# Broadcasts moved to the head of each slot, norm rows joined, and transpositions in 64-row halves, in a software-pipelined MetaFormer block

## The chip, the cores and the metric

The kernel runs on one core of one Trainium2 chip. The metric is device time in microseconds (us) of one execution; a change of less than about 0.2% can't be told from none here. The median of the kernel before is 706.19 us.

## The reference, cut to what matters

The input `x` is 4 images of 64 channels and 128 x 128 tokens. All arithmetic is in float32.

```python
def ln_c(v):                                   # over the channels
    return (v - v.mean(1)) / sqrt(v.var(1) + 1e-6)
xn = ln_c(x)
k, q = relu(Wk @ xn + bk), relu(Wq @ xn + bq)  # 8 heads of 8 channels
v = Wv @ xn + bv
context = einsum('bhkn,bhvn->bhkv', k, v)      # summed over a whole image
x1 = x + Wr @ einsum('bhkv,bhkn->bhvn', context, q) + br
t = tokens(x1)                                 # 64 channels each
n = (t - mean(t)) / sqrt(var(t) + 1e-5)
top_p, top_i = top_k(softmax(n @ router_w + router_b), 2)    # 8 experts
out = t + sum over 2 of top_p / sum(top_p) * (n @ expert_w[top_i] + expert_b[top_i])
```

## The kernel before, in words

**Tiles.** 128 partitions hold 64 channels of two stretches of an image (`s` = 0, 1). A group is 1024 tokens of each, as two units `u` of 512; there are 32 groups, 8 for each image. Of the eight PSUM banks six (`misc`) rotate: `bank_uses()` lists every use of a bank in TensorE's order, use number i has bank i mod 6, and TensorE waits (`when_free`) until the use six places back was read (`taken`).

**Steps and slots.** A loop over steps `n` runs every stage of the work on another group: the stage that lags by L steps works on group `n - L`. Each step has four slots `k`, and each engine has its own list of what it issues in a slot, in order; an engine never goes past an instruction that waits.

- Slot 3, lag 0: `measure_x` makes the rows of means and squares of x (L986), ScalarE copies them to `stat_rows` (L497). Step after, slot 0: `to_columns` turns them back (2 transpositions, L1006), ScalarE copies to `xs` (L504), and VectorE's seven small `x_deviations` (L654 to L657, `newton` at L642 to L644) give 1/deviation.
- Lag 2: slot 0 `turn_x`, 8 transpositions of 128 x 128, four for each unit (L911); VectorE `normalise`s each unit (L676) into `xnT`; slot 1 `turn_back` transposes 8 times again (L921) and ScalarE copies to `xn` (L492).
- Lag 3: slot 0 `make_keys` (L936, L943), slot 1 `sum_up` of keys against `xnT` (L974) and `add_sums` on VectorE (L688), slot 2 `make_queries` (L960). At the end of an image four `fold` steps build the attention matrix (L1030 to L1036).
- Lag 11: slot 2 `attend` (L1020) and `residual` on VectorE (L720), slot 3 `square_x1` on ScalarE. Lag 12: `route` makes the rows of the second norm and the router (L986), lag 13 their columns.
- From lag 14: 27 small VectorE steps (`gates`) choose two experts for two groups at once; `quad_in` and `gates_by_phase` lay them on eight slots, `gate_steps` lays ScalarE's square root, exponential and casts. Lag 16, slot 3: `turn_gates` (L1045), ScalarE copies to `grows` (L565).
- Lag 17, two iterations `i` in each slot (8 for a group): `broadcast(i)` spreads gate rows over 64 partitions each, two banks (L1059); for s = 0 VectorE multiplies with `x1d` out of PSUM (L816, `product`), for s = 1 ScalarE copies the bank to `gbs` (L571) and GpSimd multiplies (L431); `experts(i)` adds both products with the expert weights into `out_bank` (L1073, L1076). At the end of a unit VectorE's `result` (L826) adds x1, and SP stores. The first matmul of the next unit (L1070) waits for that.

**Order within a slot, before.** TensorE: the stages' own work, then `broadcast` for the next slot's iterations, then `experts` of this slot's. VectorE: fold, result, sums, `x_deviations`, residual, gates, `normalise`, and the slot's two products last. ScalarE: keys, columns, back, rows, then `copy_gates`, then the rest. GpSimd: the two products, and in slot 1 the squares of the next x.

Of the kernel before, what the change touches and what calls it, by code (L numbers as in the profile page):

```python
# [31 lines left out]
NLG = SE + 2 * S  # L32

# [7 lines left out]
L_COLS, L_TURN, L_KEYS, L_AGAIN, L_ATTEND, L_ROUTE, L_GATES, L_TURN_GATES, L_EXPERTS = 1, 2, 3, 9, 11, 12, 14, 16, 17  # L41
# [3 lines left out]
R_X, R_Q, R_X1, R_Z = 3, 8, 7, 4  # L45
# [17 lines left out]

def bank_uses():

    for n in range(STEPS):
        for k in range(SLOTS):
            if folding(n, k):
                yield "fold", *folding(n, k)
            if k == 0:  # L70
                if real(n - L_KEYS):
                    yield from (("keys", n - L_KEYS, s) for s in range(S))
                if real(n - L_COLS):
                    yield "stat_cols", n - L_COLS, 0
                if real(n - L_ROUTE - L_COLS):
                    yield "route_cols", n - L_ROUTE - L_COLS, 0
                if real(n - L_TURN):
                    yield from (("turned", n - L_TURN, u) for u in range(U))
            if k == 1:
                if real(n - L_KEYS):  # L80
                    yield "sums", n - L_KEYS, 0
                if real(n - L_TURN):
                    yield from (("back", n - L_TURN, u) for u in range(U))
# [5 lines left out]
            if k == 3:  # L89
                if real(n - L_TURN_GATES):  # L90
                    yield "gate_rows", n - L_TURN_GATES, 0
                if real(n):
                    yield "stat_rows", n, 0
                if real(n - L_ROUTE):
                    yield "route_rows", n - L_ROUTE, 0
            for i in iterations(n, k + 1):
                yield from (("spread", i, s) for s in range(S))
# [6 lines left out]
def constants():  # L104
# [15 lines left out]
    for s in range(S):  # L120
        for k, col in enumerate((0, S, SE, SE + S)):
            means[half == s, k, col + s] = 1.0 / C
# [14 lines left out]
def metaformer_block(nc, x, Wk, bk, Wq, bq, Wv, bv, Wr, br, router_w, router_b, expert_w, expert_b,  # L137
# [4 lines left out]
    with ExitStack() as ctx:  # L142
# [44 lines left out]
        stat_rows = sb("stat_rows", [P, U, P])  # L187
# [17 lines left out]
        route_rows = sb("route_rows", [P, U, P])  # L205
# [182 lines left out]
        def quad_in(n, k, phase):  # L388

            p, late = divmod(SLOTS * (n - L_GATES) + k - 1 - phase, 2 * SLOTS)  # L390
# [3 lines left out]
        def _(pool):  # L394
# [20 lines left out]
            def square_x(g, u):  # L415

                if u == 0:
                    pool.wait_ge(x_in[g % R_X], 32 * (g // R_X + 1))
                    if g:
                        when_filled(pool, ("stat_rows", g - 1, 0))  # L420
# [46 lines left out]
        def _(act):  # L467
# [17 lines left out]
            def take_back(g, u):  # L485

                bank = when_filled(act, ("back", g, u))
# [4 lines left out]
                nc.scalar.copy(xn[:, g % 2, u * NT:(u + 1) * NT], bank[:, :]).then_inc(taken_of(("back", g, u)), 1)  # L492

            def take_stat_rows(g):

                bank = when_filled(act, ("stat_rows", g, 0))
                nc.scalar.copy(stat_rows[:, :, :].rearrange("p u n -> p (u n)"), bank[:, 0:U * P]  # L497
                               ).then_inc(taken_of(("stat_rows", g, 0)), 1)

            def take_stat_cols(g):  # L500

                bank = when_filled(act, ("stat_cols", g, 0))
                upto(act, xstat_dve, g * N_XSTAT)
                nc.scalar.copy(xs[:, :, :], bank[:, 0:U * P].rearrange("p (a r) -> p a r", r=W)[:, :, 0:2 * S]  # L504
                               ).then_inc(taken_of(("stat_cols", g, 0)), 1)
# [6 lines left out]
            def take_route_rows(g):  # L512

                bank = when_filled(act, ("route_rows", g, 0))
                nc.scalar.copy(route_rows[:, :, :].rearrange("p u n -> p (u n)"), bank[:, 0:U * P]
                               ).then_inc(taken_of(("route_rows", g, 0)), 1)

            def take_route_cols(g):

                bank = when_filled(act, ("route_cols", g, 0))  # L520
                upto(act, gate_dve, (g // 2 - 2) * N_GATE + 8)
                half = g % 2 * U * NJ
                nc.scalar.copy(lg[:, g // 2 % 2, half:half + U * NJ, :],
                               bank[:, 0:U * P].rearrange("p (a r) -> p a r", r=W)[:, :, 0:NLG]
                               ).then_inc(taken_of(("route_cols", g, 0)), 1)

            def square_x1(g, u):

                when_taken(act, ("attended", g, u))
                if g:  # L530
                    when_filled(act, ("route_rows", g - 1, 0))
# [41 lines left out]
            gate_steps = {0: root_dev, 5: exponent, 7: high, 8: low}  # L573
# [16 lines left out]
            for n in range(STEPS):  # L590
                if n == L_TURN:
                    spread_key_bias()
                for k in range(SLOTS):
                    if k == 0:
# [3 lines left out]
                        if real(n - L_COLS):  # L598
                            take_stat_cols(n - L_COLS)
                        if real(n - L_ROUTE - L_COLS):  # L600
                            take_route_cols(n - L_ROUTE - L_COLS)
                    if k == 1 and real(n - L_TURN):
                        for u in range(U):
                            take_back(n - L_TURN, u)
                    if k == 3:
                        if real(n - L_TURN_GATES):
                            take_gate_rows(n - L_TURN_GATES)
                        if real(n):
                            take_stat_rows(n)

                    for i in iterations(n, k + 1):
                        copy_gates(i)

                    if k == 1 and real(n - L_COLS):
                        root_x(n - L_COLS)
                    if k == 2 and real(n - L_KEYS):
                        for s in range(S):
                            take_queries(n - L_KEYS, s)
                    if k == 3:
                        if real(n - L_ROUTE):  # L620
                            take_route_rows(n - L_ROUTE)
                        if real(n - L_ATTEND):
                            for u in range(U):
                                square_x1(n - L_ATTEND, u)
                    for phase, step in gate_steps.items():
# [4 lines left out]
        def _(dve):  # L630
# [18 lines left out]
            def x_deviations(g, k0, k1):  # L649
# [11 lines left out]
                for k in range(k0, k1):  # L661
                    if k == 0:
                        when_taken(dve, ("stat_cols", g, 0))
# [6 lines left out]
            def normalise(g, u):  # L670

                bank = when_filled(dve, ("turned", g, u))
# [3 lines left out]
                dve.tensor_tensor(xnT[:, g % 2, u, :, 1:P + 1].rearrange("p j (s c) -> p j s c", s=S),  # L676
                                  bank[:, :].rearrange("p (j s c) -> p j s c", j=NJ, s=S),
                                  halves(rstd[:, g % 2, u, :]).unsqueeze(3).to_broadcast([P, NJ, S, C]), ALU.mult
                                  ).then_inc(taken_of(("turned", g, u)), 1)
# [43 lines left out]
            def gates(p, k0, k1):  # L723
# [7 lines left out]
                def start():  # L731
                    for i in range(2):
                        when_taken(dve, ("route_cols", 2 * p + i, 0))
# [73 lines left out]
            gates_by_phase = {8: (26, 27), 0: (0, 4), 2: (4, 9), 3: (9, 12), 4: (12, 16), 6: (16, 20), 7: (20, 26)}  # L807
# [63 lines left out]
            for n in range(STEPS):  # L871
                if n == L_TURN:
                    set_weights()
                for k in range(SLOTS):
# [4 lines left out]
                    if k == 1:  # L879
                        if real(n - L_KEYS):  # L880
                            add_sums(n - L_KEYS)
                        if real(n - L_COLS):
                            x_deviations(n - L_COLS, 0, 4)
                    if k == 2:
                        if real(n - L_EXPERTS):
                            result(n - L_EXPERTS, 0)
                        if real(n - L_ATTEND):
                            for u in range(U):
                                residual(n - L_ATTEND, u)
                    if k == 3 and real(n - L_COLS):  # L890
                        x_deviations(n - L_COLS, 4, N_XSTAT)
                    for phase, (k0, k1) in gates_by_phase.items():
                        if quad_in(n, k, phase) is not None:
                            gates(quad_in(n, k, phase), k0, k1)
                    if k == 0 and real(n - L_TURN):
                        for u in range(U):
                            normalise(n - L_TURN, u)

                    for i in iterations(n, k + 1):
                        product(i)  # L900
# [3 lines left out]
        def _(pe):  # L904

            def turn_x(g, u):

                use = ("turned", g, u)
                bank = when_free(pe, use)
# [3 lines left out]
                ins.then_inc(filled_of(use), 1)  # L913

            def turn_back(g, u):

                use = ("back", g, u)
                bank = when_free(pe, use)
                when_taken(pe, ("turned", g, u))
# [249 lines left out]
```

## Time and profile before

| | |
|---|---|
| three runs | 705.63 to 706.54 us, median 706.19 |
| the profiled execution | 708.03 us, of which the span from the first to the last instruction is 706.2 |
| mean granted TensorE clock | 0.990 |
| busy: TensorE, VectorE, ScalarE, GpSimd | 647.4, 532.2, 428.5, 396.5 us |

Busy time of TensorE is the union of its matmuls; pipelined matmuls overlap at their ends, so starts, not durations, give the pace. "PEld" is the load of the stationary operand.

### The profile page before, as it was taken

The numbers are of one execution on the slowest core, as the hardware profiler recorded it, in microseconds if no ns is written. First come the engines' busy times: TensorE is split into PE (matmuls) and PEld (weight loads), VectorE is DVE, ScalarE is ACT, GpSimd is POOL, SyncE is SP. The second block draws the span as 40 slices with busy tenths as digits, with TensorE's granted clock in tenths as the row PEclk, the third lists the DMA queues.
The fourth block names the chain that finished last, engine by engine and source line by source line (L and its number), as shares of the span: only waits on it lengthen the run. The fifth ranks groups of instructions, "written<-read, shape, count | busy, mean of one in ns | idle before, by whom it ended". The sixth has DMA issues, their size and how long they took to land.

```text
span 706.2 us, 20616 instructions
## 1 busy us (share of the span) xinstructions
PE 647.4 (92%) x7846; PEld 302.0 (43%) x7846; DVE 532.2 (75%) x1176; ACT 428.5 (61%) x852; POOL 396.5 (56%) x350
## 2 busy tenths in 40 slices
PE   3898999799999999999999999999989889896786
PEld 1676766444544444444544444444322223231221
DVE  3443456878788988888788988867889998978853
ACT  2354556857566676657576776756656666564542
POOL 7132342165456566565456566555657667575785
PEclk9999999999999999999999999999999999999999
DMA  6232544655565555555566564444656555454442
GB/s 141 61 75 71 130 122 122 169 145 123 136 151 135 136 140 125 127 136 123 133 150 148 123 148 99 98 111 107 149 130 152 120 120 135 102 131 97 107 104 46
DMA packets 32660, 86.16 MB, mean 122 GB/s; under 512 B 7650, under 2 KB 7826, under 8 KB 32562
## 3 DMA queue, kind: packets, MB, share of 16 engines
q1 hardware_dynamic: 32082, 84.64, 50.7%
q8 instruction: 63, 1.03, 0.7%
q0 software_dynamic: 288, 0.19, 0.1%
q14 instruction: 35, 0.29, 0.1%
q10 hardware_dynamic: 192, 0.01, 0.0%
HBM read 34.47 MB, written 16.78 MB: 73 GB/s over the span
## 4 chain that ended last, share of the span: by engine, by line
PE 68%; DVE 13%; ACT 10%; issue 7%; DMA 1%; POOL 1%; DVEq 0%; SPq 0%; ACTq 0%; POOLq 0%
PE bank L1073 25%; PE bank L1059 8%; PE bank L986 5%; PE bank L921 5%; PE bank L974 5%; PE bank L943 4%; PE bank L911 4%; ACT grows L565 3%; DVE z L816 3%; PE bank L1020 3%; PE bank L1006 2%; ACT L543 2%; DVE osb L826 2%; PE bank L1070 2%; DVE x L720 2%
## 5 line engine op out<-in xcount | busy, mean ns | idle before, releaser
L431 POOL TENSOR_TENSOR z<-gbs,x1d 128x512 f32<-128x512 f32 x256 | 320.6, 1275 | 220.7 <-ACT gbs L571 164.8
L1076 PE MATMUL bank<-z,ew 128*64 128x512 f32 x512 | 248.0, 607 | 0.0
L1073 PE MATMUL bank<-z,ew 128*64 128x512 f32 x512 | 247.9, 607 | 0.0
L571 ACT COPY gbs<-bank 128x512 f32<-128x512 f32 x256 | 140.0, 593 | 95.3 <-PE bank L1059 94.4
L816 DVE TENSOR_TENSOR z<-bank,x1d 128x512 f32<-128x512 f32 x256 | 162.9, 677 | 20.4 <-PE bank L1059 20.1
L1059 PE MATMUL bank<-grows,sel 64*64 64x512 f16 x1024 | 89.3, 388 | 28.2 <-DVE z L816 17.0
L422 POOL TENSOR_TENSOR xsq<-xin 128x512 f32<-128x512 f32 x64 | 65.6, 1046 | 81.8 <-DMA xin<-in_x_dram 78.2
L1073 PEld LDWEIGHTS bank<-z,ew 128*64 128x64 f32 x512 | 65.7, 138 | 105.6 <-issue 95.8
L492 ACT COPY xn<-bank 128x512 f32<-128x512 f32 x64 | 34.6, 588 | 68.2 <-PE bank L921 68.2
L676 DVE TENSOR_TENSOR xnT<-bank,rstd 128x512 f32<-128x512 f32 x64 | 41.3, 684 | 39.2 <-PE bank L911 37.0
L1059 PEld LDWEIGHTS bank<-grows,sel 64*64 64x64 f16 x1024 | 24.1, 104 | 97.2 <-issue 34.4
L1076 PEld LDWEIGHTS bank<-z,ew 128*64 128x64 f32 x512 | 65.6, 138 | 0.0
L826 DVE TENSOR_TENSOR osb<-bank,x 128x512 f32<-128x512 f32 x64 | 43.8, 685 | 23.1 <-PE bank L1076 23.1
L565 ACT COPY grows<-bank 128x1024 f16<-128x1024 f16 x32 | 32.3, 1010 | 30.3 <-PE bank L1045 30.3
L474 ACT ACTIVATE keys<-bank 128x512 f32<-128x512 f32 x64 | 34.8, 595 | 25.4 <-PE bank L943 25.4
L720 DVE SCALAR_TENSOR_TENSOR x<-bank,br_col,x_again 128x512 f32<-128x512 f32 x64 | 44.9, 743 | 5.2 <-PE bank L1020 4.8
L482 ACT ACTIVATE q<-bank,bq_col 128x512 f32<-128x512 f32 x64 | 40.6, 689 | 7.2 <-PE bank L960 7.2
L974 PEld LDWEIGHTS bank<-xnT,keys 128*64 128x64 f32 x1024 | 34.7, 139 | 13.3 <-issue 12.2
L974 PE MATMUL bank<-xnT,keys 128*64 128x66 f32 x1024 | 36.7, 225 | 1.2 <-ACT keys L474 1.0
L921 PE MATMUL bank<-k,xnT 128*128 128x128 f32 x256 | 35.9, 284 | 1.7 <-DVE xnT L676 1.2
L532 ACT ACTIVATE x1sq<-x 128x512 f32<-128x512 f32 x64 | 37.4, 645 | 0.0
L943 PEld LDWEIGHTS bank<-wk_bd,xn 64*64 64x64 f32 x2048 | 35.5, 135 | 4.2 <-issue 1.9
(138 smaller groups left out, 885.0 us busy)
## 6 DMA issues: line engine op xcount, KB each, us to landing
x1d<-x SPq DMA_DIRECT2D x128, 256.0 KB, 4.5
xin<-in_x_dram SPq DMA_DIRECT2D x64, 256.0 KB, 4.1
x_again<-in_x_dram SPq DMA_DIRECT2D x64, 256.0 KB, 4.1
out_dram<-osb SPq DMA_DIRECT2D x128, 128.0 KB, 2.4
k<-in_const_dram SPq DMA_DIRECT2D x1, 453.5 KB, 3.7
ew_nat<-in_L_ffn_expert_w_dram POOLq DMA_DIRECT2D x2, 64.0 KB, 6.5
sel<-in_const_sel_dram SPq DMA_DIRECT2D x1, 128.0 KB, 3.5
bk_rows<-bk_wide ACTq DMA_DIRECT2D x6, 1.0 KB, 1.7
```

The source lines that it names most:

```text
L422: pool.tensor_tensor(xsq[:, u * NT:(u + 1) * NT], half, half, ALU.mult).then_inc(x_squared, 1)
L431: pool.tensor_tensor(z[:, 1, i % R_Z, :], gbs[:, i % R_Z, :], x1d[:, g % 2, 1, u * NT:(u + 1) * NT], ALU.mult).then_inc(z_pool, 1)
L571: nc.scalar.copy(gbs[:, i % R_Z, :], bank[:, :]).then_inc(taken_of(("spread", i, 1)), 1)
L720: dve.scalar_tensor_tensor(x1[:, g % R_X1, half], bank[:, :], br_col[:, 0:1], x_again[:, g % 2, half], ALU.add, ALU.add).then_inc(taken_of ...
L816: dve.tensor_tensor(z[:, 0, i % R_Z, :], bank[:, :], x1d[:, g % 2, 0, u * NT:(u + 1) * NT], ALU.mult).then_inc(taken_of(("spread", i, 0)), 1)
L826: dve.tensor_tensor(osb[:, g % 2, half], out_bank[:, :], x1[:, g % R_X1, half], ALU.add).then_inc(out_done, 1)
L921: ins = pe.transpose(bank[:, j * P:(j + 1) * P], xnT[:, g % 2, u, j, 1:P + 1], eye)
L943: ins = pe.matmul(banks[s][C * a:C * a + C, j * C:(j + 1) * C], xn[rows, g % 2, j * P + C * a:j * P + C * a + C], wk_bd[rows, rows], start ...
L974: ins = pe.matmul(bank[C * s:C * s + C, 0:C + 2], keys[:, s, at:at + C], xnT[:, g % 2, u, j, C * s:C * s + C + 2], start=(u == 0 and j == ...
L1059: ins = pe.matmul(bank[cols, :], sel[rows, j, cols], grows[rows, g % 2, u * NT:(u + 1) * NT], start=True, stop=True)
L1073: pe.matmul(out_bank[0:C, :], ew[:, j, :], z[:, 0, i % R_Z, :], start=False, stop=(j == PAIRS - 1), skip_group_check=True).then_inc(prod_d ...
L1076: pe.matmul(out_bank[C:P, :], ew[:, j, :], z[:, 1, i % R_Z, :], start=False, stop=(j == PAIRS - 1), skip_group_check=True).then_inc(prod_d ...
```

## The change

1. **Order in a slot.** TensorE issues `broadcast` first, before folds and stages. ScalarE's `copy_gates` comes first too. VectorE: fold, result, `x_deviations` and the gate steps 26, 0 to 3 and 4 to 6 (`gates_first`, these from SBUF but for 26) before the products; `normalise`, `add_sums`, `residual` and the other gate steps behind them. In slot 1 `turn_back` now comes before `sum_up`.
2. **Gates two slots later**, `turn_gates` at lag 17, slot 1, and the experts at lag 18: 50 steps where there were 49, with eight buffers of `x1` for seven.
3. **Joined rows.** Rows of x and of x1 go to one bank, one `rows_sb` and one pair of transpositions: where both exist one ScalarE copy and two transpositions less per step.
4. **Halves.** `turn_x` and `turn_back` transpose 64 rows at a time, 16 transpositions of 64 rows by 128 columns of which the two row halves alternate and write two banks. Both banks are full only at the end, and `normalise` and `take_back` work on a row half in place of a unit.

```diff
@@ bank_uses, and the same order in the TensorE loop @@
+            for i in iterations(n, k + 1):
+                yield from (("spread", i, s) for s in range(S))
             if folding(n, k):
...
-            for i in iterations(n, k + 1):
-                yield from (("spread", i, s) for s in range(S))
@@ VectorE loop @@
+                    for phase, (k0, k1) in gates_first.items():
+                        if quad_in(n, k, phase) is not None:
+                            gates(quad_in(n, k, phase), k0, k1)
+                    for i in iterations(n, k + 1):
+                        product(i)
+                    if k == 0 and real(n - L_TURN):
+                        for s in range(S):
+                            normalise(n - L_TURN, s)
+                    if k == 1 and real(n - L_KEYS):
+                        add_sums(n - L_KEYS)
+                    if k == 2 and real(n - L_ATTEND):
...
-            gates_by_phase = {8: (26, 27), 0: (0, 4), 2: (4, 9), 3: (9, 12), 4: (12, 16), 6: (16, 20), 7: (20, 26)}
+            gates_first = {8: (26, 27), 0: (0, 4), 2: (4, 7)}
+            gates_by_phase = {2: (7, 10), 3: (10, 11), 4: (11, 16), 5: (16, 18), 6: (18, 24), 7: (24, 26)}
-            gate_steps = {0: root_dev, 5: exponent, 7: high, 8: low}
+            gate_steps = {0: root_dev, 4: exponent, 7: high, 8: low}
@@ TensorE @@
-            def turn_x(g, u):
...
-                for j in range(NJ):
-                    ins = pe.transpose(bank[:, j * P:(j + 1) * P],
-                                       xin[:, g % R_X, u * NT + j * P:u * NT + (j + 1) * P], eye)
+            def turn_x(g):
+                uses = [("turned", g, s) for s in range(S)]
+                banks = [when_free(pe, use) for use in uses]
+                for a in range(U * NJ):
+                    for s in range(S):
+                        rows = slice(C * s, C * s + C)
+                        ins = pe.transpose(banks[s][:, a * C:(a + 1) * C], xin[rows, g % R_X, a * P:(a + 1) * P],
+                                           eye[rows, rows])
+                        if a == U * NJ - 1:
+                            ins.then_inc(filled_of(uses[s]), 1)
...
+            def to_columns(n):
...
+                when_taken(pe, ("rows", n, 0))
                 for u in range(U):
-                    ins = pe.transpose(bank[:, u * P:(u + 1) * P], rows[:, u, :], eye)
+                    ins = pe.transpose(bank[:, u * P:(u + 1) * P], rows_sb[:, u, :], eye)
...
                     if k == 1:
+                        if real(n - L_TURN_GATES):
+                            turn_gates(n - L_TURN_GATES)
+                        if real(n - L_TURN):
+                            turn_back(n - L_TURN)
                         if real(n - L_KEYS):
                             sum_up(n - L_KEYS)
```

## Rows read from the trace of the kernel before

**Rows 1.** The page: busy time, and the chain that ended last.

```profile
PE 647.4 (92%) x7846; PEld 302.0 (43%) x7846; DVE 532.2 (75%) x1176; ACT 428.5 (61%) x852; POOL 396.5 (56%) x350
...
PE 68%; DVE 13%; ACT 10%; issue 7%; DMA 1%; POOL 1%; DVEq 0%; SPq 0%; ACTq 0%; POOLq 0%
```

**Rows 2.** Three stretches: window, length, busy us of each engine, clock, DMA, GB/s.

```profile
0.00:142.40 142.40, 122.66 (x2225) 82.45 (x2225) 71.31 (x230) 75.54 (x170) 46.61 (x64) 0.99 0.47 113
142.40:439.40 297.00, 291.92 (x3670) 140.07 (x3672) 247.97 (x541) 197.99 (x398) 180.12 (x151) 1.00 0.56 133
439.40:706.20 266.80, 232.77 (x1953) 79.48 (x1949) 212.91 (x408) 154.98 (x286) 169.77 (x136) 0.98 0.49 115
```

**Rows 3.** TensorE's timeline in a full step: start, us, engine, line, shapes, count.

```profile
301.91 1.10 PE L943 MATMUL bank<-wk_bd,xn 64*64 64x64 f32 x64
...
303.22 0.38 PE L1006 MATMUL bank<-k,route_rows 128*128 128x128 f32 x2
303.43 1.04 PE L911 MATMUL bank<-k,xin 128*128 128x128 f32 x8
304.40 0.63 PE L1059 MATMUL bank<-grows,sel 64*64 64x512 f16 x8
...
313.16 0.60 PE L1059 MATMUL bank<-grows,sel 64*64 64x512 f16 x6
...
314.31 0.41 PE L1070 MATMUL bank<-grows,eb_rows 128*64 128x512 f16 x2
...
318.24 0.61 PE L986 MATMUL bank<-x1sq,k 128*32 128x256 f32 x8
318.95 0.63 PE L1059 MATMUL bank<-grows,sel 64*64 64x512 f16 x8
319.50 0.64 PE L1073 MATMUL bank<-z,ew 128*64 128x512 f32 x1
```

**Rows 4.** Timeline of an early step, TensorE and VectorE.

```profile
62.28 1.09 PE L960 MATMUL bank<-xn,wq 64*64 64x512 f32 x8
...
65.84 1.04 PE L911 MATMUL bank<-k,xin 128*128 128x128 f32 x8
66.48 1.29 DVE L676 TENSOR_TENSOR xnT<-bank,rstd 128x512 f32<-128x512 f32 x2 [2.72 <-PE bank L911]
68.00 1.09 PE L921 MATMUL bank<-k,xnT 128*128 128x128 f32 x8
69.02 1.09 PE L960 MATMUL bank<-xn,wq 64*64 64x512 f32 x8
```

**Rows 5.** ScalarE's timeline: gate rows in slot 3 of steps 39, 40 and 41.

```profile
569.09 1.01 ACT L565 COPY grows<-bank 128x1024 f16<-128x1024 f16 x1
586.06 1.01 ACT L565 COPY grows<-bank 128x1024 f16<-128x1024 f16 x1 [2.24 <-PE bank L1045]
599.11 1.01 ACT L565 COPY grows<-bank 128x1024 f16<-128x1024 f16 x1
```

**Rows 6.** Timeline of step 40, TensorE and VectorE.

```profile
579.76 1.19 DVE L777 TENSOR_TENSOR bstat<-bstat,lg 128x32 f32<-128x32 f32 x1
...
582.16 0.41 PE L1059 MATMUL bank<-grows,sel 64*64 64x512 f16 x4 [1.49 <-DVE z L816]
```

**Rows 7.** Line L777: durations in ns, min/median/max.

```profile
L777 DVE TENSOR_TENSOR bstat<-bstat,lg x16: 191/192/1195, 116.0 to 641.4; 128x32 f32<-128x32 f32 x16
```

**Rows 8.** Columns as in rows 2, three microseconds of step 42.

```profile
614.00:617.00 3.00, 3.00 (x9) 0.49 (x5) 2.86 (x8) 0.00 (x0) 1.86 (x2) 0.50 0.39 87
```

**Rows 9.** Two pairs of weight loads, from the timeline of PEld.

```profile
178.04 0.29 PEld L1032 LDWEIGHTS bank<-wvT,sT_sb 64*128 64x128 f32 x2 [0.81 <-ACT q L482]
...
302.94 0.20 PEld L1006 LDWEIGHTS bank<-k,stat_rows 128*128 128x128 f32 x2
```

**Rows 10.** ScalarE's timeline: rows of x in slot 3 of steps 14 and 16.

```profile
118.94 0.37 ACT L497 COPY stat_rows<-bank 128x256 f32<-128x256 f32 x1
...
140.85 0.41 ACT L497 COPY stat_rows<-bank 128x256 f32<-128x256 f32 x1
```

More of the change, by code:

```diff
@@ L32 @@
 NLG = SE + 2 * S
+NROW = NLG + 2 * S
 PPB = HW // (S * NP)
@@ L88, in bank_uses @@
                     yield from (("queries", n - L_KEYS, s) for s in range(S))
[L89 to L95, printed above, removed]
-            for i in iterations(n, k + 1):
-                yield from (("spread", i, s) for s in range(S))
+            if k == 3 and has_rows(n):
+                yield "rows", n, 0
 ROUND = 6
@@ L593, in _ @@
                 for k in range(SLOTS):
+                    for i in iterations(n, k + 1):
+                        copy_gates(i)
                     if k == 0:
@@ L878, in _ @@
                         result(n - L_EXPERTS - 1, 1)
[L879 to L889, printed above, removed]
+                    if k == 1 and real(n - L_COLS):
+                        x_deviations(n - L_COLS, 0, 4)
+                    if k == 2 and real(n - L_EXPERTS):
+                        result(n - L_EXPERTS, 0)
                     if k == 3 and real(n - L_COLS):
                         x_deviations(n - L_COLS, 4, N_XSTAT)
+                    for phase, (k0, k1) in gates_first.items():
+                        if quad_in(n, k, phase) is not None:
+                            gates(quad_in(n, k, phase), k0, k1)
+                    for i in iterations(n, k + 1):
+                        product(i)
[5 more added lines that the diff above has]
+                    if k == 2 and real(n - L_ATTEND):
+                        for u in range(U):
+                            residual(n - L_ATTEND, u)
                     for phase, (k0, k1) in gates_by_phase.items():
@@ L894, in _ @@
                             gates(quad_in(n, k, phase), k0, k1)
[L895 to L900, printed above, removed]
             result(GROUPS - 1, 1)
@@ L977, in sum_up, with make_rows @@
                 ins.then_inc(filled_of(use), 1)
-            def rows_of(use, tile, squares, w, w_square):
+            def make_rows(n):
+                use = ("rows", n, 0)
                 bank = when_free(pe, use)
-                outs = [bank[W * j:W * (j + 1), 0:U * P].rearrange("p (u n) -> p u n", u=U) for j in range(NJ)]
-                for moving, weights, start in ((tile, w, True), (squares, w_square, False)):
-                    chunks = moving.rearrange("p (u j n) -> p u j n", u=U, j=NJ)
+                parts = []
+                if real(n):
+                    pe.wait_ge(x_in[n % R_X], 32 * (n // R_X + 1))
+                    pe.wait_ge(x_squared, (n + 1) * U)
+                    parts += [(xin[:, n % R_X, :], mean_w), (xsq[:, :], square_w)]
+                g = n - L_ROUTE
+                if real(g):
+                    pe.wait_ge(x1_squared, (g + 1) * U)
+                    parts += [(x1[:, g % R_X1, :], route_w[:, :]), (x1sq[:, :], route_square_w)]
+                for part, (tile, weights) in enumerate(parts):
+                    chunks = tile.rearrange("p (u j n) -> p u j n", u=U, j=NJ)
@@ L985, in rows_of @@
                     for j in range(NJ):
-                        ins = pe.matmul(outs[j], weights, chunks[:, :, j, :], start=start, stop=not start,
-                                        skip_group_check=True)
+                        out_rows = bank[W * j:W * (j + 1), 0:U * P].rearrange("p (u n) -> p u n", u=U)
+                        ins = pe.matmul(out_rows, weights, chunks[:, :, j, :], start=(part == 0),
+                                        stop=(part == len(parts) - 1), skip_group_check=True)
@@ L1103, in _ @@
                 for k in range(SLOTS):
+                    for i in iterations(n, k + 1):
+                        broadcast(i)
                     if folding(n, k):
```

179 lines of the change are left out of this document (76 added, 103 removed).

## The prediction

> **What bounds the kernel now.** I read the page first: TensorE is busy 92% of the span and makes 68% of the chain that ended last, but a fifth of that chain is VectorE and ScalarE [rows 1]. A share like that hides stages, so I cut the span into three by the experts' start and the last group's entry [rows 2]. Steps 0 to 16 (up to 142.4) have no experts: TensorE is busy 123 of 142 us, most of the rest at the start. Steps 17 to 31 are full: 297 us for 15 steps, 19.8 each, TensorE busy 98%, VectorE 16.5 us a step. From 439.4 the x stages drain and 17 steps take 266.8 us, TensorE 87% and VectorE 80% busy.
>
> Then the timelines. In a full step TensorE is never idle for long, but two places are slack although they look busy, because the ends of pipelined matmuls cover them. The two broadcasts of a slot take 0.55 us (318.95 to the experts at 319.50), in slot 2 they take 1.15 (313.16 to 314.31): 0.60 lost, for the banks which `residual` frees. And the last rows matmul, 0.43 long by its neighbours' spacing, starts at 318.24, the broadcast only at 318.95: 0.28 lost, for `grows` [rows 3]. An early step, 6.74 us (62.28 to 69.02), has no gap: VectorE starts on the first unit at 66.48 while TensorE still transposes the second, is done at 67.77, and `sum_up` fills the time until `turn_back` at 68.00 [rows 4]. A late step takes 17.0 or 13.0 us by turns (569.09, 586.06, 599.11), 30.0 a pair [rows 5]. The long ones are even: there VectorE has most gate steps ahead of its products, and TensorE waits 1.49 us for a product's bank [rows 6]. Some of these small SBUF steps last 1.19 us where their median is 0.19 [rows 7]; in the timeline the long ones lie beside a GpSimd product. In step 42, after the same two waits, TensorE's granted clock is at the lower level, 1.2 GHz, for at least 3 us [rows 8].
>
> **Halved transpositions.** 8 transpositions of 128 moving columns take 0.97 us from start to next start (303.43 to 304.40), 0.107 each and some 0.1 for the change of shape [rows 3]. With 64 moving columns and the row halves side by side a pair should take 0.055: that matmuls of 64 columns in four quarters of the array keep such a pace is seen at L943, 64 of them in 1.03 us (301.91 to 302.94), 0.064 for four [rows 3]. The question is the weight load, which keeps 128 columns. The load pair of L1006, transpositions, lasts 0.20 with 0.14 for one, so it starts 0.06 apart; that of L1032, ordinary float32 weights of 64 rows by 128 columns, 0.29 with 0.18 for one, starts 0.11 apart [rows 9]. The nearest row is the transposition's: I take 0.055 a pair, 8 x (0.107 - 0.055) = 0.42 us less for each of `turn_x` and `turn_back`, 0.84 a step. Bounds: nothing, if loads of a pair follow one another or take 0.11; and +0.85 each (16 x 0.11 = 1.76) if the halves neither load nor multiply side by side and each load takes 0.11.
>
> The Trainium skill ("TensorE: Matmul & The Clock Gate", LDWEIGHTS) has the load's time go by its columns alone, 128 / 1.2 = 107 ns, however few the rows. By it a pair takes 0.107 and the turns save nothing. The trace agrees for L1032 and not for L1006 [rows 9].
>
> **Joined rows.** The rows' matmuls stay. The second pair of transpositions, 0.21 us (303.22 to 303.43) [rows 3], goes in steps where both exist, 13 to 31. The ScalarE copy that goes is hidden anyway.
>
> **Broadcasts first, gates later.** In a full step the 0.60 and the 0.28 go: the broadcasts' banks were read a slot earlier, and `grows` is copied two slots ahead. So TensorE alone would need 19.70 - 0.88 - 0.21 - 0.84 = 17.8. But VectorE has 16.5 a step [rows 2], with its order against it. In slot 0 both halves of `normalise` (1.29) start only after all of `turn_x`; `x_deviations` follow, then slot 1's products, and `turn_back` needs the bank of the first: I draw 0.3 us of waiting in odd steps, 0.7 in even ones. `add_sums` now stands behind `turn_back` and `sum_up` and blocks VectorE for about 1.2 us; in even steps six gate steps (2.5 us) queue behind it, then `result` and slot 2's products, and `make_queries` waits about 0.8 to 1.6 for their bank. Odd steps 18.1, even 19.7; 19.0 with what long SBUF steps add. 14 full steps (one fewer) make 266 where 15 made 297: **-31**.
>
> **Early steps.** Here the move of `turn_back` costs. Only `to_columns` (about 0.25) lies between it and `turn_x`. VectorE starts when all 16 are done, works 1.29, and `turn_back` starts some 1.2 us late, with nothing of TensorE's to cover it. Net +1.2 - 0.84 = +0.36, in steps 2 to 14: +4.7, less 0.4 for the join. Steps 15 and 16 took 21.9 us with gates in them [rows 10]; now 15, 16 and 17 have them, VectorE-bound at about 10.6 each, 32: +10. Together **+14.3**: full steps start near 156.7.
>
> **Late steps, 32 to 49.** TensorE needs 12.7 (the 13.0 of an odd step less its waits), VectorE was busy 212.9 / 17 = 12.5 a step over all late steps [rows 2], the last of which lack gates and `residual`; where it has them I take 13.4, an estimate. But its gate steps now lie behind the products and more evenly over slots (at most 2.5 us in one). I draw one chain left: even slot 1's gates, `result` in slot 2, the first matmul of the next unit; about 2.3 us a pair. 13.9 a step for 35 to 42, so 27.8 a pair where it was 30.0 [rows 5]. Steps 32 to 34: 18.2, 17.6, 16.3. Step 43: 12.6; 44 to 46: 12.5 each, VectorE's gates; 47 to 49: 10.8 each, near what GpSimd's 8 products need (169.8 / 17 = 10.0 [rows 2]), and 2 for the end. Sum 52.1 + 111.2 + 12.6 + 37.5 + 34.4 = 247.8, against 266.8: **-19**.
>
> Sum: 14.3 - 31 - 19 = -35.7. The profiled execution took 708.0 and would take 672.3; it is 1.8 over the median, so 670.5 for the median, say **670**.
>
> **Hidden at nothing.** The stores, loads and x1d copies move in SP's queue with their conditions, each a step ahead of its reader; DMA is about half busy in all three stretches [rows 2]. Moving `copy_gates` first on ScalarE costs nothing while ScalarE has a third of its time free; `exponent`, one slot earlier, waits for the last gate step of its own slot and holds the next slot's copies about 0.7 us, covered by the slot between a product and its experts. If that cover is gone TensorE waits the 0.7 once in 2 steps: 11 us in all.
>
> **Rivals.**
> - *Turns save nothing* (loads 0.11 a pair or one after another). For: L1032's load; by the Trainium skill's rule on load columns (TensorE page, LDWEIGHTS) this is what happens. Against: L1006's. Early steps +0.84 x 15 = 12.6; full steps 19.5, as VectorE's chain hides part, +7: **690**. Chance 0.2.
> - *VectorE stays the bound.* Its chains cost in every step what they cost in even ones: full steps 19.6 (+8), late pairs 30.0 (+9): **687**. For: 16.5 us busy in a full step, and the blocked `add_sums`. Against: most gate steps now leave the way of the products. Chance 0.13.
> - *Slower: the halves serialise.* A turn of 1.76 us instead of 0.5, 64 turns, +1.25 each, 80 us less what full and late steps hide: **about 730**. It decides from 1.05 us a turn on, against 0.97 before: (706 - 670) / 64 = 0.56 over my 0.5. For: no row shows transpositions of 64 rows. Against: L943's four quarters. Chance 0.05.
> - *Better than drawn.* The waits of slots 1 and 2 do not come, full steps 18: **655**. Chance 0.1.
>
> The forecast has 0.52. Its own range is 661 to 680. Within 0.2%, which is what a measurement here can tell, lies almost none: 0.02; slower 0.06 (the third rival and an unseen wait), faster 0.92. Leaving out the last rival's lower half and the slower one, the range is 654 to 693.
>
> **What would show it.** After: 16 transpositions in about 0.5 us, loads in pairs; an early step near 7.1 us with TensorE waiting about 1.2 for `normalise`; full steps near 19.0 with waits at `turn_back` and `make_queries` in even ones, none at broadcasts; late pairs near 28; fewer falls of the clock. Wrong it would be by the turn's length first, worth 6.4 us for each 0.1, then by the early wait, 1.2 x 15 = 18 us.

## The result and the profile after

The changed kernel takes 749.92 us (746.78 to 751.62, 4 runs), the kernel before 706.37 us (705.63 to 708.09, 4 runs): ratio 1.0604, 95% interval 1.057 to 1.0637. It is 43.5 us slower where 36 us less was forecast. In order: the page of the profiled execution (span 747.2 us), then its three stages, cut at the same work as in [rows 2] (the rows' copies of steps 17 and 31, before of 16 and 31).

```profile
PE 642.1 (86%) x8318; PEld 283.8 (38%) x8318; DVE 534.8 (72%) x1176; ACT 421.5 (56%) x832; POOL 398.4 (53%) x350
...
PE 56%; DVE 26%; issue 10%; ACT 4%; DVEq 0%; ACTq 0%
```

```profile
0.00:156.60 156.60, 122.36 (x2647) 78.36 (x2647) 77.82 (x249) 80.95 (x181) 50.57 (x68) 0.98 0.44 109
156.60:464.20 307.60, 273.47 (x3616) 123.01 (x3618) 233.13 (x508) 181.18 (x359) 169.57 (x141) 0.95 0.50 120
464.20:747.20 283.00, 246.27 (x2057) 82.45 (x2053) 223.90 (x421) 159.40 (x296) 178.26 (x143) 0.95 0.48 114
```

No engine has much more work; TensorE is idle for 105 us where it was for 59, and VectorE's share of the chain doubled [rows 1]. The mean clock fell from 0.990 to 0.958: (1 - 0.958) x 2 x 747.2 = 63 us at the 1.2 GHz level, 14 before. The forecast had 156.7, 266 and 247.8 for the stages: the first is right to 0.1 us, the second 41.6 too short, the third 35.2.

An ordinary full step, TensorE's timeline, as in [rows 3]:

```profile
271.09 0.40 PE L1059 MATMUL bank<-grows,sel 64*64 64x512 f16 x2
271.90 0.41 PE L1059 MATMUL bank<-grows,sel 64*64 64x512 f16 x4 [0.40 <-DVE z L806]
272.49 0.40 PE L1059 MATMUL bank<-grows,sel 64*64 64x512 f16 x2 [0.18 <-DVE z L806]
272.71 0.41 PE L936 MATMUL bank<-bk_rows,ones 64*64 64x512 bf16 x4
...
273.98 0.71 PE L905 MATMUL bank<-k,xin 64*128 64x64 f32 x16
274.62 0.44 PE L1006 MATMUL bank<-k,rows_sb 128*128 128x128 f32 x2
274.99 0.41 PE L1070 MATMUL bank<-grows,eb_rows 128*64 128x512 f16 x2
...
290.56 0.63 PE L1059 MATMUL bank<-grows,sel 64*64 64x512 f16 x8
```

A turn takes 0.64 us start to start (273.98 to 274.62). From L936 to the next step's broadcasts TensorE has no wait: 17.85 us, and with these broadcasts (290.56 to the next L936 at 291.02) 18.3. But the broadcasts at the head of this step, an odd one (23), take 1.6 (271.09 to 272.71), for banks that products hold. The even step behind it waits 0.40 us before `turn_x` and 1.12 before `make_queries`, and not before `turn_back`. Ordinary pairs of full steps took 39.4, forecast 37.8 to 38.0, before 39.3.

The worst place is a step that folds. Step 27, TensorE and VectorE in order of time, and below it TensorE's clock (0.57) from 356 to 364:

```profile
354.46 0.41 PE L1059 MATMUL bank<-grows,sel 64*64 64x512 f16 x4 [1.49 <-DVE z L806]
...
357.45 0.64 PE L936 MATMUL bank<-bk_rows,ones 64*64 64x512 bf16 x4 [1.62 <-issue]
...
364.29 0.63 PE L1059 MATMUL bank<-grows,sel 64*64 64x512 f16 x8
...
364.84 0.43 PE L1036 MATMUL bank<-wrT,ctxT_sb 64*128 64x64 f32 x2
...
365.31 0.29 DVE L696 COPY att<-bank 128x128 f32<-128x128 f32 x1 [3.14 <-PE bank L1036]
365.44 2.48 POOL L430 TENSOR_TENSOR z<-gbs,x1d 128x512 f32<-128x512 f32 x2 [7.29 <-ACT gbs L563]
365.52 1.21 DVE L642 SCALAR_TENSOR_TENSOR xstat<-xs 128x16 f32<-128x16 f32 x1
...
366.76 1.19 DVE L643 TENSOR_TENSOR xstat<-xstat,xs 128x16 f32<-128x16 f32 x1
...
370.33 1.28 DVE L806 TENSOR_TENSOR z<-bank,x1d 128x512 f32<-128x512 f32 x2
...
371.07 1.12 PE L919 MATMUL bank<-k,xnT 64*128 64x64 f32 x16 [5.25 <-DVE z L806]
```

```profile
356.00:364.00 8.00, 6.55 (x96) 4.10 (x96) 3.23 (x6) 1.60 (x5) 2.15 (x2) 0.57 0.20 43
```

VectorE is in its list at the fold's last step (L696), whose TensorE half now stands behind the broadcasts. It waits 3.14 us, then `x_deviations` come out while GpSimd multiplies (1.21 and 1.19 us for steps that take 0.17 otherwise), and only then the product, at 370.33, whose bank `turn_back` needs: TensorE idles 5.25 us. The pair of steps 18 and 19 took 54.7 us, 26 and 27 took 56.1, where other full pairs take 39.4: 32 us. Before, a pair with folds cost 1.3 more than another. Steps 34 and 35 hold folds too.

A late even step, the end of slot 2 and slot 3 of step 40:

```profile
614.93 0.63 PE L1059 MATMUL bank<-grows,sel 64*64 64x512 f16 x8
...
615.71 0.43 DVE L788 TENSOR_TENSOR bank<-bank,bstat 128x256 f32<-128x256 f32 x1
...
616.18 1.07 ACT L544 CAST gT<-bank 128x256 f16<-128x256 f32 x2 [3.56 <-DVE bank L788]
...
617.14 1.09 ACT L563 COPY gbs<-bank 128x512 f32<-128x512 f32 x2
617.35 0.70 DVE L738 TENSOR_TENSOR bank<-bank,gT 128x512 f32<-128x512 f32 x1 [1.21 <-ACT gT L544]
...
617.96 1.23 DVE L723 SCALAR_TENSOR_TENSOR bstat<-lg 128x32 f32<-128x32 f32 x1
...
620.93 1.22 DVE L806 TENSOR_TENSOR z<-bank,x1d 128x512 f32<-128x512 f32 x2
...
621.61 0.41 PE L1059 MATMUL bank<-grows,sel 64*64 64x512 f16 x4 [2.85 <-DVE z L806]
```

ScalarE's cast (`high`) stands at the end of slot 2 and waits for gate steps 24 and 25 of that same slot, which now stand behind its products. So it waits 3.56 us, holds slot 3's copy of the gates (its broadcasts stand ready from about 615.5, the copy starts at 617.14), and VectorE waits for it in turn at step 26, ahead of slot 3's products; then steps 0 to 3 lie beside GpSimd's product. TensorE waits 2.85. From step 36 on late pairs took 31.3 to 32.7, forecast 27.8, before 30.0 [rows 5] and, from step 40 on, 31.7.

### The profile page after: what moved, and what is told of

Read it like the earlier page. It is cut to its first block, busy times and chain, and to the rows that moved or that the text cites. A ratio compares the mean times of both kernels' runs of the same rounds, so it can differ in the third digit from the quotient of the medians.

```text
span 747.2 us, 21530 instructions
## 1 busy us (share of the span) xinstructions
PE 642.1 (86%) x8318; PEld 283.8 (38%) x8318; DVE 534.8 (72%) x1176; ACT 421.5 (56%) x832; POOL 398.4 (53%) x350
## 4 chain that ended last, share of the span: by engine, by line
PE 56%; DVE 26%; issue 10%; ACT 4%; DVEq 0%; ACTq 0%
PE bank L1073 18%; PE bank L1059 6%; DVE z L806 6%; PE bank L974 5%; PE bank L996 5%; PE bank L960 3%; PE bank L919 3%; PE bank L943 3%; PE bank L1070 3%; PE bank L905 3%; PE bank L1020 3%; DVE x L709 2%; DVE bstat L766 2%; DVE bstat L723 2%; DVE osb L816 2%
## 5 line engine op out<-in xcount | busy, mean ns | idle before, releaser
L1076 PE MATMUL bank<-z,ew 128*64 128x512 f32 x512 | 252.8, 618 | 0.0
L1073 PE MATMUL bank<-z,ew 128*64 128x512 f32 x512 | 252.7, 618 | 0.0
L563 ACT COPY gbs<-bank 128x512 f32<-128x512 f32 x256 | 138.4, 591 | 151.1 <-PE bank L1059 150.9
L1073 PEld LDWEIGHTS bank<-z,ew 128*64 128x64 f32 x512 | 67.6, 142 | 99.6 <-issue 81.7
L664 DVE TENSOR_TENSOR xnT<-bank,rstd 128x512 f32<-128x512 f32 x64 | 41.2, 685 | 55.0 <-PE bank L905 53.7
L1059 PEld LDWEIGHTS bank<-grows,sel 64*64 64x64 f16 x1024 | 21.1, 105 | 139.2 <-issue 100.5
L1076 PEld LDWEIGHTS bank<-z,ew 128*64 128x64 f32 x512 | 67.6, 142 | 0.0
L919 PE MATMUL bank<-k,xnT 64*128 64x64 f32 x512 | 24.5, 238 | 27.8 <-DVE xnT L664 14.8
L960 PE MATMUL bank<-xn,wq 64*64 64x512 f32 x256 | 35.3, 621 | 6.3 <-DVE z L806 6.3
L1020 PE MATMUL bank<-q,att 64*64 64x512 f32 x256 | 35.3, 627 | 5.6 <-issue 5.6
L943 PEld LDWEIGHTS bank<-wk_bd,xn 64*64 64x64 f32 x2048 | 38.7, 145 | 3.3 <-issue 0.5
L974 PE MATMUL bank<-xnT,keys 128*64 128x66 f32 x1024 | 39.5, 234 | 0.0
```

The costliest lines, as they stand in the source:

```text
L563: nc.scalar.copy(gbs[:, i % R_Z, :], bank[:, :]).then_inc(taken_of(("spread", i, 1)), 1)
L943: ins = pe.matmul(banks[s][C * a:C * a + C, j * C:(j + 1) * C], xn[rows, g % 2, j * P + C * a:j * P + C * a + C], wk_bd[rows, rows], start ...
L960: ins = pe.matmul(banks[s][cols, :], wq_4[rows, cols], xn[rows, g % 2, u * NT:(u + 1) * NT], start=True, stop=True)
L974: ins = pe.matmul(bank[C * s:C * s + C, 0:C + 2], keys[:, s, at:at + C], xnT[:, g % 2, u, j, C * s:C * s + C + 2], start=(u == 0 and j == ...
L1059: ins = pe.matmul(bank[cols, :], sel[rows, j, cols], grows[rows, g % 2, u * NT:(u + 1) * NT], start=True, stop=True)
L1073: pe.matmul(out_bank[0:C, :], ew[:, j, :], z[:, 0, i % R_Z, :], start=False, stop=(j == PAIRS - 1), skip_group_check=True).then_inc(prod_d ...
```

## The experiments

The result and its trace left three theories of the 80 us between forecast and result: the gate steps set ahead of the products (A), `turn_back` ahead of `sum_up` (B), the broadcasts ahead of the folds (C). Each experiment has its ratio to the kernel before as timed beside it (median 706.14 us for e1 to e4, 705.06 for e5 to e8, 705.35 for e9 to e12).

**e1: all gate steps behind the products.**

```diff
-            gates_first = {8: (26, 27), 0: (0, 4), 2: (4, 7)}
-            gates_by_phase = {2: (7, 10), ...
+            gates_by_phase = {8: (26, 27), 0: (0, 4), 2: (4, 10), ...
```

> The changed kernel with gate steps 26, 0 to 3 and 4 to 6 behind the slot's products, as all others (x_deviations stay ahead). Theory A (these steps, with the wait for ScalarE's casts in step 26 and the SBUF steps that meet GpSimd's products, hold the products of every second step's slot 3, so that TensorE waits 2 to 3 us for banks and its clock falls): waits of L1059 for L806's product fall from 24 us to under 8, time at the low clock from some 63 us to under 25, time 715 to 725. Theory B (turn_back ahead of sum_up is what costs, early and in fold steps): 745 to 750, early step still 7.2 us. Theory C (fold behind the broadcasts): 740 to 750, steps 18, 19, 26 and 27 still 27 us each.

760.14 us (755.65 to 762.06), ratio 1.0784 (1.0743 to 1.0826): slower by 10. Theory A falls: ahead of the products is the better place for them. The size is not of the place alone, for step 26, which ScalarE's `low` waits for, moved too; e11 below moves the others without it.

**e2: `sum_up` ahead of `turn_back` again**, in TensorE's loop and the banks' order.

```diff
+                        if real(n - L_KEYS):
+                            sum_up(n - L_KEYS)
                         if real(n - L_TURN):
                             turn_back(n - L_TURN)
-                        if real(n - L_KEYS):
-                            sum_up(n - L_KEYS)
```

> The changed kernel with sum_up ahead of turn_back again, in TensorE's order and in the order of banks. Theory B: the early step goes from 7.2 to about 6.3 us (15 of them, 13 us), the 5 us waits of turn_back in fold steps shrink, 720 or less. Theory A: only the early steps gain, 733 to 738, late steps unchanged at about 31.5 a pair.

730.66 us (727.13 to 731.24), ratio 1.0375 (1.035 to 1.04): 19 us back. Early steps take 6.6 us on average for 7.2, ordinary full pairs 38.4 for 39.4, the pairs with folds 50.8 and 54.5 for 54.7 and 56.1.

**e3: the fold ahead of the broadcasts again.**

```diff
+                    if folding(n, k):
+                        fold(*folding(n, k))
                     for i in iterations(n, k + 1):
                         broadcast(i)
-
-                    if folding(n, k):
-                        fold(*folding(n, k))
```

> The changed kernel with a slot's fold ahead of its broadcasts, in TensorE's order and in the order of banks, as it stands in VectorE's. Theory C (VectorE, whose fold step comes first in its slot, waits 3 us for a fold that TensorE issues behind four broadcasts): fold steps fall from 27 to about 22 us each, 725 to 732. Theory A: the wait for the fold falls by the broadcasts' 0.6 us, but steps 26 and 0 to 3 still stand ahead, 742 to 750.

723.79 us (720.56 to 727.21), ratio 1.0278 (1.0237 to 1.0319): 26 us back. The pairs with folds fall from 54.7 and 56.1 to 44.9 and 45.0, that of steps 34 and 35 from 36.4 to 32.5, the clock rises to 0.975, and ordinary pairs stay. C is confirmed. This order makes 21 of the 32 us of steps 18, 19, 26 and 27; their pairs still cost 5.6 more than others.

**e4: the kernel before with halved transpositions alone** (part 4, `sum_up` first as it was).

```diff
-                                turn_x(n - L_TURN, u)
+                            turn_x(n - L_TURN)
...
-                                turn_back(n - L_TURN, u)
+                            turn_back(n - L_TURN)
```

> The kernel before with nothing changed but the transpositions in 64-row halves (sum_up still ahead of turn_back). Turns take 0.5 us for 0.97: full steps 18.9 for 19.8 (15 of them, 12 us), early steps some 0.4 less (6 us): 685 to 692. If the halves cost somewhere else (clock, normalise later), 700 to 712.

702.07 us (698.37 to 706.26, 10 runs), ratio 0.9945 (0.9914 to 0.9976): 4 us, not the 14 to 21 expected. Full pairs are 38.6 for 39.3. Why the rest of what the turns save does not show in the time stays open.

**e5: e2 and e3 together.**

> The changed kernel with both orders of before back inside a slot: sum_up ahead of turn_back, and the fold ahead of the broadcasts. If their costs are separate, both gains (19 and 26 us) add up: 703 to 707 us, fold pairs 42 to 45 us, early steps 6.5 to 6.8, pairs of full steps 38.4. If they are largely the same loss (the waiting of a fold step is also a wait of turn_back), the sum is 712 to 718. Late pairs stay at 31 to 32 either way, which leaves the kernel no faster than before.

705.29 us (702.56 to 706.26, 10 runs), ratio 1.0 (0.9983 to 1.0017): the two losses add up (19.3 + 26.1 = 45.4, and e5 gives 44.6). Pairs with folds take 41.4 or 41.5 for 38.4 of the others. Late pairs stay at 31.6 to 32.8.

**e6: e5, and no gate step in the slot of the cast or exponential that waits for it.**

```diff
-            gates_by_phase = {2: (7, 10), 3: (10, 11), 4: (11, 16), 5: (16, 18), 6: (18, 24), 7: (24, 26)}
+            gates_by_phase = {2: (7, 10), 3: (10, 16), 5: (16, 20), 6: (20, 26)}
```

> As e5, with the gate steps that ScalarE waits for one slot before it wants them: steps 10 to 15 in phase 3 (exponent in phase 4), 16 to 19 in phase 5, 20 to 25 in phase 6 (high in phase 7). Theory: late pairs grew from 30.0 to 31.5 because ScalarE's exponent and high wait for steps of their own slot that stand behind the products, and hold the next slot's copies of gates: then late pairs fall by 1 to 1.5 us and the time is 8 to 14 us below e5. Rival: late steps are bound by VectorE's own work in the slots whatever the phases: within 3 us of e5, or slower, since phase 3 and 6 now hold six steps.

686.73 us (682.9 to 690.75), ratio 0.9733 (0.9681 to 0.9786): 18.6 us less, more than expected. Late pairs are 27.8 to 27.9, from the rows of ScalarE; full pairs stay at 38.4. The edit moves the gate steps of `exponent` as well as those of `high`. ScalarE waits before both: 18.8 us before the first cast in e5 and 4.0 in e6, 1.8 before the exponential and then nothing. So most of the gain goes with `high`, but no run moves one without the other. The line of the first cast, from the groups by line, in the changed kernel and in e6 (busy, mean ns, idle before and its releaser):

```profile
L544 ACT CAST gT<-bank 128x256 f16<-128x256 f32 x16 | 6.0, 373 | 22.0 <-DVE bank L788 21.7
```

```profile
L544 ACT CAST gT<-bank 128x256 f16<-128x256 f32 x16 | 5.9, 372 | 4.0 <-DVE bank L788 4.0
```

In a late step of e6 the cast waits 0.83 and starts before the next copy of gates is due; step 26 waits for nothing:

```profile
588.28 1.07 ACT L544 CAST gT<-bank 128x256 f16<-128x256 f32 x2 [0.83 <-DVE bank L788]
...
591.27 0.69 DVE L738 TENSOR_TENSOR bank<-bank,gT 128x512 f32<-128x512 f32 x1
591.43 1.07 ACT L563 COPY gbs<-bank 128x512 f32<-128x512 f32 x2 [2.08 <-PE bank L1059]
```

**e7: e5 with transpositions in 128 rows** (part 4 undone; the edit is e4's, reversed).

> As e5, but with turn_x and turn_back in 128 rows, each unit with its own bank, as before (part 4 of the change undone). If a halved turn is worth 0.4 us also here: 4 to 12 us above e5, early steps 6.7 (of which sum_up covers the wait). If the halves' late start of normalise (both banks full only at the end) eats what they save: within 3 us of e5, or below it.

714.34 us (714.01 to 715.59), ratio 1.0127 (1.0102 to 1.0153): 9 us more than e5. The halves gain here too, most in odd full steps (20.1 for 19.5, between the rows' copies).

**e8: e4 with joined rows** (parts 3 and 4 on the kernel before; `rows_of` gives way to `make_rows`).

```diff
-                            take_stat_rows(n)
...
-                            take_route_rows(n - L_ROUTE)
+                            take_rows(n)
```

> The kernel before with parts 3 and 4 alone (halved transpositions and joined rows) and its own order and gate phases. The join drops two transpositions (0.21 us) in 19 steps and an extra ScalarE copy: 3 to 5 us less than e4's 702, so 697 to 699 us, if the rows copy stays hidden. Rival: joined rows wait for both the squares of x and of x1 and their copy waits behind them: no gain or up to 5 us slower in late or full steps.

700.27 us (698.17 to 702.85, 8 runs), ratio 0.9933 (0.9905 to 0.9961): 1.8 us below e4 (0.8 by the ratios), not distinguishable from it by the intervals.

**e9: the changed kernel with e6's gate phases alone.**

> The changed kernel with the gate phases of e6 alone (no gate step that ScalarE waits for stands in the slot of its cast or exponential), and its own orders of TensorE. If the casts are a loss of their own, they are worth here what they were worth beside the other two edits, 18.6 us: 730 to 733 us, late pairs 28 to 29. If half of that was fewer falls of the clock, which the folds of this kernel bring anyway: 736 to 742.

731.69 us (730.3 to 736.9), ratio 1.0398 (1.034 to 1.0457): 18.2 us less than the changed kernel, as beside the other two edits (18.6). The loss stands by itself.

**e10: e8 with its gate steps spread in the same way**, and `exponent` in phase 4 for 5.

```diff
-            gates_by_phase = {8: (26, 27), 0: (0, 4), 2: (4, 9), 3: (9, 12), 4: (12, 16), 6: (16, 20), 7: (20, 26)}
+            gates_by_phase = {8: (26, 27), 0: (0, 4), 2: (4, 10), 3: (10, 16), 5: (16, 20), 6: (20, 26)}
```

> e8 (the kernel before with halved transpositions and joined rows, 700.3 us) with the same spread of its gate steps: 10 to 15 in phase 3 and exponent in phase 4, 16 to 19 in phase 5, 20 to 25 in phase 6. In the kernel before ScalarE waits for gate steps too (13.6 us in all before its casts to gT in late steps), but there the broadcasts of a slot come last, so its copies have more cover. Theory: it gains part of it, 692 to 697 us, and stays above e6's 686.7. Rival: with products behind the gate steps the six steps of phase 3 and of phase 6 delay products more: 700 to 706.

681.49 us (679.66 to 682.81), ratio 0.9671 (0.9626 to 0.9715): the fastest kernel of the study, 18.8 below e8 where 3 to 8 were expected. The kernel before had the wait too: 15.1 us in all at the first cast, here 2.2. Its late pairs are 28.1.

**e11: e6 with gate steps 0 to 6 behind the products** (26 stays ahead).

```diff
-            gates_first = {8: (26, 27), 0: (0, 4), 2: (4, 7)}
-            gates_by_phase = {2: (7, 10), ...
+            gates_first = {8: (26, 27)}
+            gates_by_phase = {0: (0, 4), 2: (4, 10), ...
```

> e6 with gate steps 0 to 3 and 4 to 6 behind the products of their slots (26 stays ahead, since low waits for it). In e6's trace steps 0 to 3 take 2.9 us ahead of a product (1.16 and 1.20 beside a GpSimd product for two of them), and the next broadcast waits 0.9 for that product's bank once in two steps. Theory: SBUF steps ahead of the products are a loss, and e1, which had them behind, was slower only because ScalarE's low waited for step 26 behind the products: now 680 to 685 us. Rival: wherever they stand they take the same time of VectorE, 685 to 690 us; if e1's loss comes from their place itself, 695 or more.

722.01 us (720.73 to 723.51), ratio 1.0248 (1.0201 to 1.0295): 35 us slower than e6. My theory and the mild rival were wrong. Steps 4 to 6, groups by line, first e6, then e11:

```profile
L632 DVE SCALAR_TENSOR_TENSOR bstat<-bstat 128x32 f32<-128x32 f32 x16 | 6.0, 375 | 0.5
...
L631 DVE TENSOR_TENSOR bstat<-bstat 128x32 f32<-128x32 f32 x16 | 5.1, 319 | 0.6
L630 DVE SCALAR_TENSOR_TENSOR bstat<-bstat 128x32 f32<-128x32 f32 x16 | 2.4, 151 | 0.0
```

```profile
L631 DVE TENSOR_TENSOR bstat<-bstat 128x32 f32<-128x32 f32 x16 | 14.3, 895 | 0.6
L632 DVE SCALAR_TENSOR_TENSOR bstat<-bstat 128x32 f32<-128x32 f32 x16 | 13.6, 847 | 0.5
L630 DVE SCALAR_TENSOR_TENSOR bstat<-bstat 128x32 f32<-128x32 f32 x16 | 13.3, 828 | 0.0
```

The same three steps take 41.2 us for 13.5. The timeline of e11, VectorE and TensorE, and below it GpSimd's:

```profile
219.02 1.26 DVE L630 SCALAR_TENSOR_TENSOR bstat<-bstat 128x32 f32<-128x32 f32 x1
...
220.32 0.96 DVE L631 TENSOR_TENSOR bstat<-bstat 128x32 f32<-128x32 f32 x1
...
221.31 0.97 DVE L632 SCALAR_TENSOR_TENSOR bstat<-bstat 128x32 f32<-128x32 f32 x1
...
223.59 0.68 DVE L816 TENSOR_TENSOR osb<-bank,x 128x512 f32<-128x512 f32 x1
224.19 1.28 DVE L806 TENSOR_TENSOR z<-bank,x1d 128x512 f32<-128x512 f32 x2
...
224.92 1.23 PE L960 MATMUL bank<-xn,wq 64*64 64x512 f32 x8 [2.17 <-DVE z L806]
```

```profile
217.72 2.51 POOL L430 TENSOR_TENSOR z<-gbs,x1d 128x512 f32<-128x512 f32 x2 [1.77 <-ACT gbs L563]
220.19 2.05 POOL L421 TENSOR_TENSOR xsq<-xin 128x512 f32<-128x512 f32 x2
222.41 2.67 POOL L430 TENSOR_TENSOR z<-gbs,x1d 128x512 f32<-128x512 f32 x2 [0.18 <-ACT gbs L563]
```

GpSimd multiplies from 217.72 to 222.24 without a gap. Behind the products steps 4 to 6 fall into that stretch, push `result` and the next products back, and `make_queries` waits 2.17 us. Ahead of them they run, in e6, mostly while GpSimd still waits for its own gates (median 0.13 to 0.19 us). Steps 0 to 3 are no part of this: they take 29.6 us in all in e11 and 35.1 in e6. Each of the three steps shown ends 0.05 us after the end of a GpSimd instruction (220.23, 221.23, 222.23). That is in line with the Trainium skill ("SBUF — State Buffer", SBUF: two separate sides): a VectorE instruction with two SBUF inputs and a GpSimd one that reads SBUF exclude each other, for the whole of an instruction.

**e12: e11 with `x_deviations` behind the products as well.**

> e11 with x_deviations behind the products as well. Theory: its seven steps (0.9 us in slot 1, 0.6 in slot 3, more beside a GpSimd product) no longer delay a product; full pairs 37.8 for 38.4, fold pairs 1 us less, together 2 to 8 us below e11. Rival: normalise in slot 0 needs them, and they would end too late behind slot 3's products: TensorE waits before turn_back, 2 to 8 us above e11.

782.56 us (777.82 to 783.83), ratio 1.1094 (1.1023 to 1.1164): another 60 us, full pairs 50. The rival had the sign, and about a tenth of the size. The seven steps of `x_deviations` take 105.7 us in all for 56.1 in e11. How much of e11's and e12's loss is the longer steps and how much the order (`result` waits behind them, `normalise` needs the deviations) no run separates.

## Why the prediction was wrong

By the runs the changed kernel is put together like this: 686.7 (e6) + 18.6 (casts) + 18.5 (`turn_back` ahead of `sum_up`, e3 less e5) + 26.1 (folds behind broadcasts) = 749.9. These are differences of successive runs, so they must add up; what supports them is that e9 gives 18.2 for the second and e2 19.3 for the third from the other side. What I left out stands in the second and fourth term; the third I had priced. Point by point:

- **Halved turns: right, a little small.** Forecast 0.42 us less each; measured 0.97 to 0.64, 0.33 less. The two of a pair start 0.003 us apart and the next pair 0.063 behind them (273.981 to 274.466 for the first to the last pair), where I took 0.055; the rest of the 0.64 is the change of shape. "About 0.5" had left that out. The rival that the halves serialise was wrong, and so was that they save nothing. The Trainium skill ("TensorE: Matmul & The Clock Gate", LDWEIGHTS) has a load's time go by its columns alone; eight pairs would need an estimated 0.86 us by it. The trace does not agree: it shows 0.64.
- **Joined rows: small, as forecast.** Two transpositions take 0.37 us (274.62 to 274.99); 1.8 us in all (e8 against e4), inside the uncertainty.
- **Early steps: right; stage one right with luck in it.** An early step takes 7.20 us for 7.1, and TensorE waits 1.10 for `normalise` where I took 1.2. But e2 gives back only 0.6 a step: with `sum_up` first the step is 6.6 and not 6.1, so the order alone costs half of what I priced. And that stage one is 156.6 for 156.7 is in part chance. Step 7 of the execution before took 10.3 us for 6.8: a pause of 1.79 us within `make_keys`, then transpositions at half the pace, the granted clock at 0.50 from 58 to 60, the 1.2 GHz level. I added my changes onto these 3.5 us, and the execution after has no such step; without them the same sum gives 153.2. First the two rows of before, then an early step of after:

```profile
57.14 0.27 PE L943 MATMUL bank<-wk_bd,xn 64*64 64x64 f32 x1 [1.79 <-issue]
...
57.80 1.91 PE L911 MATMUL bank<-k,xin 128*128 128x128 f32 x8
```

```profile
50.66 0.71 PE L905 MATMUL bank<-k,xin 64*128 64x64 f32 x16
...
51.41 1.29 DVE L664 TENSOR_TENSOR xnT<-bank,rstd 128x512 f32<-128x512 f32 x2 [3.19 <-PE bank L905]
...
52.85 0.70 PE L919 MATMUL bank<-k,xnT 64*128 64x64 f32 x16 [1.10 <-DVE xnT L664]
...
53.48 1.16 PE L974 MATMUL bank<-xnT,keys 128*64 128x66 f32 x32
```

- **"14 full steps make 266": the first failing step.** It multiplied one ordinary step by 14. Four of them hold folds, whose order against the broadcasts the diff turns round; I described the folds and priced them at nothing. 32 of the 41.6 us are there. Their order against the broadcasts is 21 of these 32 (e3), 5 more come back when `sum_up` stands first as well (e5), and 6 stay, against 2.6 before. In e5, with both old orders, the stage takes 274.8, in e6 277.3.
- **"TensorE alone 17.8": too low.** The rows give 18.3. 0.18 us of it is the two turns and 0.09 the columns' transpositions (0.49 to 0.37 where I took off 0.21); for the rest, a subtraction of slack that overlapping matmuls had partly covered, I have no row. "None at broadcasts" is wrong too: 1.6 us for 0.56 at the head of odd steps. These and the 0.40 before `turn_x` are 2.5 us a pair; the waits of 0.3 and 0.7 drawn at `turn_back`, which ordinary pairs do not have, take 1.0 off again, and about 1.4 is left.
- **"I draw one chain left": the second failing step.** 27.8 us a late pair can be had: e6 has it (27.8 to 27.9). But I had counted gate steps "behind the products and more evenly" as a gain and not asked who waits for them. I did ask it of `exponent` (0.7 us, "11 us in all" uncovered), and not of `high`, which stands in the same line of the diff's table and holds the copies of gates. Measured price: 18.4 us, by e6 and e9, with `exponent`'s part in it (1.8 us of ScalarE's waits, against 21.7 before the first cast). Of the 12 us that e6's last stage (260.0) is still above the forecast, 7.8 are in steps 44 to 49, drawn at 71.9 and taking 79.7.
- **"Fewer falls of the clock": wrong.** 63 us at the lower level for 14. By an estimate at half clock that is up to 31 us of matmul time against 7, so up to 24 of the 43.5 us came by way of the clock, after waits as in step 27. It is not a cause of its own: e6, with most of the waits gone, has 0.992.
- **Not weighed at all: what early gate steps are worth.** I had read that long SBUF steps lie beside GpSimd's products [rows 7], and made no term of it. Set behind the products, gate steps 0 to 6 cost e6 35 us (e11). It is no gain of the change: the kernel before has all its gate steps ahead of its products, and its steps 4 to 6 take 10.2 us in all, those of e6 13.5.
- The rival on the slower side had the right sign by another mechanism. None of my rivals was a fold or a cast.

Parts 3 and 4 alone are worth 5 us of the kernel before (e8), the spread gate phases 19 (e10). Set beside e10 (681.49), e6 (686.73) shows that broadcasts first with gates two slots later, even repaired, bring nothing that these runs can show.

## What to carry to other kernels

When a block of work moves within the engines' lists, go through every stage that it passes, the rare ones too: four steps with folds among 14 lost 32 us, where the ordinary ones gained nothing. For each instruction that moves later, name who waits for it on the other engines and what stands behind that waiter in its list; put a producer one slot ahead of its reader. Small VectorE steps out of SBUF belong where GpSimd is idle.

## What the runs showed of the hardware

- Sixteen float32 transpositions of 64 rows in two alternating row halves take 0.64 us to the next start. Pairs start 0.063 us apart, the two of a pair 0.003, though every load keeps 128 columns; the transpositions of 128 rows start 0.109 apart (step 25 before, 303.43 to 304.20).
- A VectorE step of 128x32 from SBUF takes 0.13 to 0.19 us alone (`newton`'s three in e6) and up to 1.26 beside GpSimd's 128x512 product; VectorE's own product, with one input in PSUM, keeps its 0.64 beside it (224.19 in e11: two in 1.28, GpSimd busy from 222.41 to 225.08).
- In step 27 TensorE waits 1.49 us up to 354.46 and 1.62 up to 357.45; the granted clock falls between 356 and 357 and is 0.57 from 356 to 364, mostly its 1.2 GHz level, and `make_keys` there takes 1.95 us for 1.13. So a wait is paid a second time by the matmuls behind it.
